# Attention a of a four-layer kernel: programs reordered in each step, and eight steps in a round of the loop

## The reference, cut to what matters

```python
topk = max(1, int(Tx * 0.3))                       # 76 of 256
qkv = x @ W_qkv.T + b_qkv                          # 16 heads of 8 features
scores = einsum('bhid,bhjd->bhij', q, k) * scale
topk_scores, indices = top_k(scores, topk)
masked = full_like(scores, -inf).at[..., indices].set(topk_scores)
out = einsum('bhij,bhjd->bhid', softmax(masked), v)
return out @ W_out.T + b_out
```

## Time and profile before

| what | us |
|---|---|
| median of 3 executions | 5544.91 (5527.25 to 5550.4) |
| the profiled execution's own time | 5548.73 |
| its span | 5547.0 |
| TensorE busy | 4738.9 (85%) |
| VectorE busy | 4094.9 (74%) |
| ScalarE busy | 3148.7 (57%) |
| GpSimd busy | 2516.4 (45%) |
| attention a in the span | about 90 to 2810 |

### The profile page before, as it was taken

The page is one execution under the profiler, slowest core; times in us unless marked ns, Lnnn a source line. Parts: engine busy times, 40 slices in busy tenths (PEclk is TensorE's granted clock), DMA queues, the critical chain, the costliest instruction groups (busy, mean ns, idle before and its releaser), DMA issues. The chain is left out here.

```text
span 5547.0 us, 121740 instructions
## 1 busy us (share of the span) xinstructions
PE 4738.9 (85%) x34686; PEld 3322.2 (60%) x34686; DVE 4094.9 (74%) x14487; ACT 3148.7 (57%) x10145; POOL 2516.4 (45%) x3026
## 2 busy tenths in 40 slices
PE   4578788788786887887889999989999998999998
PEld 2244444444443444444468888866666666888887
DVE  3788888888887888888958888855555554788886
ACT  3587777677775777777622222257667776222222
POOL 0465555565554555656644444421111111444444
PEclk6566665565665566667589999999999999999999
DMA  2000000000000000000023443410000000434344
GB/s 67 10 13 10 10 13 10 10 13 9 10 13 7 13 10 10 13 10 12 7 58 81 84 85 81 89 24 10 10 10 12 10 10 9 92 77 91 78 87 98
DMA packets 358589, 188.51 MB, mean 34 GB/s; under 512 B 190691, under 2 KB 346886, under 8 KB 358150
## 3 DMA queue, kind: packets, MB, share of 16 engines
q1 hardware_dynamic: 358150, 183.55, 16.4%
HBM read 147.04 MB, written 11.01 MB: 28 GB/s over the span
## 5 line engine op out<-in xcount | busy, mean ns | idle before, releaser
L845 ACT ACTIVATE junk<-SS,nt 128x256 bf16<-128x256 f32 x3072 | 1515.4, 502 | 188.4 <-POOL nt L481 113.3
L493 POOL TENSOR_SCALAR gone<-SS,mid 128x256 bf16<-128x256 f32 x1024 | 1193.0, 1180 | 664.3 <-DVEq L1039 533.2
L1206 POOL TENSOR_TENSOR f_hid<-f_g_m,f_cbs 128x256 f32<-128x256 f32 x1024 | 743.4, 726 | 853.2 <-DVE f_g_m L1451 660.6
L1306 ACT ACTIVATE f_th<-bank 128x256 f32<-128x256 f32 x1088 | 417.1, 383 | 1149.0 <-PE bank L1237 1149.0
L1236 PE MATMUL bank<-f_xTf,wgT 128*128 128x256 f32 x2176 | 692.3, 400 | 54.3 <-DVE f_g_m L1451 38.6
L668 PE MATMUL bank<-q4x,k4x 32*128 32x256 f32 x2048 | 526.2, 603 | 224.4 <-DVE SS L961 186.9
L1852 DVE TENSOR_REDUCE nmxb<-bank 128x2 f32<-128x512 f32 x512 | 330.1, 688 | 474.6 <-PE bank L1624 474.6
L1237 PE MATMUL bank<-f_xTf,wuT 128*128 128x256 f32 x2176 | 651.5, 381 | 0.0
L1268 PEld LDWEIGHTS bank<-wdT,f_hid 128*128 128x128 f32 x4096 | 601.5, 191 | 66.9 <-POOL f_hid L1206 12.5
L1268 PE MATMUL bank<-wdT,f_hid 128*128 128x128 f32 x4096 | 629.6, 276 | 10.5 <-POOL f_hid L1206 10.4
L845 ACT ACTIVATION_READ_ACCUMULATOR junk<-SS,nt 128x1 f32 x3072 | 599.5, 195 | 0.0
(11 more groups left out here) (233 smaller groups left out, 8134.9 us busy)
## 6 DMA issues: line engine op xcount, KB each, us to landing
f_cbs<-f_shares SPq DMA_DIRECT2D x512, 256.0 KB, 5.8
q4x<-q SPq DMA_DIRECT2D x64, 256.0 KB, 2.3
k4x<-k SPq DMA_DIRECT2D x64, 128.0 KB, 2.1
qrow<-q_rows SPq DMA_DIRECT2D x512, 8.0 KB
q_rows<-qTb SPq DMA_DIRECT2D x32, 128.0 KB, 1.7
out_dram<-xres SPq DMA_DIRECT2D x4, 1024.0 KB, 9.3
q4x<-nmx_rows SPq DMA_DIRECT2D x128, 4.0 KB
f_shares<-f_combT SPq DMA_DIRECT2D x64, 32.0 KB, 1.4
```

Of the source, the lines that this page charges most:

```text
L493: last = pool.tensor_scalar(gone[:, h % 4, i, :], SS[:, (u - lag) % 4, c, :], mid[:, (u - lag) % 4, c:c + 1], 0.0, ALU.subtract, ALU.min)
L845: nc.scalar.activation(junk[:, c % 2, :], SS[:, uu % 4, c, :], ACT.Sign, bias=bias(c), accum_out=acc[:, k, uu % 4, c:c + 1]).then_inc(s["s ...
L1206: pool.tensor_tensor(hid[:, e % NBUF, :], g_m[:, e % NBUF, :], cbs[:, par, e, :], ALU.mult).then_inc(s["hid"], 1)
```

## The change

1. `schedule` writes steps -1 to 7 out, runs steps 8 to 55 in 6 rounds of eight steps, and writes steps 56 to 67 out.
2. TensorE: in a quarter the four scores of the next group come first, then (quarter 2) `project(1)` or `spreads`, then `below_max` and `remove`, then `weigh` of the pair before (`SUMS`), then the guests. `turn_sums` moves from quarter 3 of a step to quarter 0 of the next, `turn_x` from quarter 1 to 0, `turn_o` from quarter 0 to 1, `q_rows` to quarter 0 behind `turn_sums`, `moments` and `queries` of the even step and `values` of the odd step behind `first_scores`.
3. ScalarE: the pairs of exponentials come at h = 2, 4, 6, 8 in place of 1, 3, 5, 7; the copy of the sums at h = 8 in place of 6, `oT` at 4 in place of 1, `take_qn` at 8 in place of 7, `take_v` at h = 8 of the odd step in place of h = 0 of the even one.
4. VectorE: `normalise` at h = 2 in place of 0, `take_k` at 7 in place of 6, `take_qr` at 3 in place of 2, `take_mom` at 5 in place of 4, the addition of y at 7 in place of 6.
5. GpSimd: `front` ahead of `outsiders(3, (6, 7))`.
6. The order of uses of M0 and M1 follows (`USES`): `gram` moves to M1, `oT` to M0.

```diff
-        USES = ({"v": 0, "xT": -1, "q0": -1, "q1": -1, "k": -1, "qn": -1, "gram": -1, "qtok": -1, "mom": -1},
-                {"f0": 1, "ktok": -1, "n0": 2, "oT": 2, "f1": 1, "y": 2, "n1": 1})
+        USES = ({"xT": -1, "q0": -1, "q1": -1, "k": -1, "qn": -1, "qtok": -1, "oT": 2, "mom": -1, "v": -1},
+                {"n0": 2, "f0": 1, "ktok": -1, "gram": -1, "n1": 2, "f1": 1, "y": 2})
...
-        BODY = (1, BATCH // 2 - 1)
+        SUMS = ((3, 0), (3, 2), (3, 4), (3, 6))
+        STEPS = 8
+        BODY = (1, GROUPS // STEPS - 1)
...
-            for u in range(4):
-                step(u, 0, u)
+            for t in range(STEPS):
+                step(t, t // 2, t % 4)
             with eng.Fori(*BODY) as i:
-                for u in range(4):
-                    step(i * 4 + u, i * 2 + u // 2, u)
...
+                for n in range(STEPS):
+                    step(i * STEPS + n, i * (STEPS // 2) + n // 2, n % 4)
+            for t in range(STEPS * BODY[1], GROUPS + 4):
+                step(t, t // 2, t % 4)
...
-                    outsiders(3, (6, 7))
                     if even and ahead:
                         front(bb + 1)
+                    outsiders(3, (6, 7))
...
-                        wait(pe, s["oc"], t - 2)
+                        wait(pe, s["oc"], t - 3)
                         use1(m1_before(bb, "n0" if even else "n1"))
...
-                        ahead = d < 3 and runs(t, -1)
-                        n = 2 * d + 2
-                        if ahead:
+                        if d < 3 and runs(t, -1):
+                            n = 2 * d + 2
                             free_bank(t + 1, n + 1)
+                            for i in range(HALVES):
+                                score(n, u + 1, i)
+                                score(n + 1, u + 1, i)
+                        if d == 2 and front:
+                            if even:
+                                project(1, m0_before(bb, "q1"))
+                            else:
+                                wait(pe, s["m1c"], m1_before(bb, "gram") + 1)
+                                spreads(m0_before(bb, "mom"))
                         if runs(g):
                             wait(pe, s["turned"], TURNED * (g + 1))
                             wait(pe, s["pt"], 8 * g + a)
-                        for k in range(2):
-                            if runs(g):
+                            for k in range(2):
                                 below_max(v, a, k)
                                 below_max(v, a + 1, k)
-                            if ahead:
-                                score(n, u + 1, k)
-                                score(n + 1, u + 1, k)
...
+                        late, a = SUMS[d]
+                        weigh(t - late, (u - late) % 4, a)
+                        if d == 0:
+                            if runs(t, 4):
+                                turn_sums()
+                            if front and even:
+                                turn_x(bb + 1, m0_before(bb, "xT"))
+                            if front and not even:
+                                q_rows(m0_before(bb, "qtok"))
+                        if d == 1:
+                            if not even and tail:
+                                turn_o()
+                            if runs(t, 2):
+                                judged()
+                            if front and even:
+                                project(0, m0_before(bb, "q0"))
+                        if d == 2:
+                            if front and even:
+                                k_rows(m1_before(bb, "ktok"))
+                                project(2, m0_before(bb, "k"))
+                            if not even and tail:
+                                project_o()
+                        if d == 3:
+                            if even and front:
+                                wait(pe, s["m0c"], m0_before(bb, "k") + 1)
+                            if runs(t, -2):
+                                first_scores(t + 2, u + 2)
+                            if even and front:
+                                moments(m1_before(bb, "gram"))
+                                queries(m0_before(bb, "qn"))
+                            if front and not even:
                                 values(m0_before(bb, "v"))
...
-                        if h % 2 == 1:
-                            late, a = PAIRS[h // 2]
+                        if h >= 2 and h % 2 == 0:
+                            late, a = PAIRS[h // 2 - 1]
                             exponentials(t - late, a)
                             exponentials(t - late, a + 1)
...
+                        if not even and front and h == 8:
+                            take_v(bb + 1, m0_before(bb, "v"))
+                        if h == 8 and runs(t, 3):
                             wait(act, s["pv"], 4 * (t - 2))
...
-                        if h == 0 and runs(t, 4):
+                        if h == 2 and runs(t, 4):
                             normalise()
...
-                        if front and even and h == 6:
+                        if front and even and h == 7:
                             take_k(m1_before(bb, "ktok"))
```

More of the change, by code:

```diff
@@ L389, in before @@
                 return b * len(order) + first - sum(max(lag, 0) for lag in order.values()) + list(order).index(what)
-            n = first
-            for c in range(b + 1):
+            n = 0
+            for c in range(-1, b + 1):
                 for o, lag in order.items():
@@ L626, in _ @@
                 k_rows(0)
-                wait(pe, s["m1c"], 1)
-                for n, f in enumerate((moments, q_rows, spreads)):
-                    f(5 + n)
+                q_rows(5)
+                moments(1)
+                wait(pe, s["m1c"], 2)
+                spreads(6)
+                values(7)
                 def rows(h):
@@ L685, in weigh @@
                             wait(pe, s["oc"], g)
-                            pe.wait_ge(s["vput"], bb)
+                            wait(pe, s["vput"], bb - 1 if even else bb)
                         for k in range(HALVES):
@@ L770, in step @@
-                        weigh(g, v, a)
-                        if even and front:
-                            if d == 1:
-                                project(0, m0_before(bb, "q0"))
-                            if d == 2:
-                                project(2, m0_before(bb, "k"))
-                            if d == 3:
-                                queries(m0_before(bb, "qn"))
-                        if not even and front and d == 0:
-                            wait(pe, s["m0c"], m0_before(bb, "qn") + 1)
-                            q_rows(m0_before(bb, "qtok"))
@@ L781, in step @@
-                    if even and front:
-                        wait(pe, s["m0c"], m0_before(bb, "k") + 1)
-                    if runs(t, -2):
-                        first_scores(t + 2, u + 2)
+                        late, a = SUMS[d]
[7 more added lines that the diff above has]
+                                q_rows(m0_before(bb, "qtok"))
@@ L822, in _ @@
                 take_qn(4)
+                take_v(0, 7)
                 own.end()
@@ L863, in step @@
                             count(t, k, u, bias, ready, done, range(CUTS[k][j], CUTS[k][j + 1]))
-                        if h == 0 and even and runs(bb, 0, BATCH):
-                            take_v(bb, m0_before(bb, "v"))
                         if even and front:
@@ L1020, in normalise @@
                     def normalise():
-                        n1 = m1_before(bb - 1, "n1") if even else m1_before(bb, "n0")
+                        n1 = m1_before(bb, "n0" if even else "n1")
                         wait(dve, s["m1"], n1 + 1)
```

81 lines of the change are left out of this document (24 added, 57 removed).

## The result

| | before | after |
|---|---|---|
| median, us | 5547.65 (5527.25 to 5553.43, 4 runs) | 5475.2 (5474.23 to 5481.61, 4 runs) |
| ratio | | 0.9878, 95% interval 0.9852 to 0.9905 |
| span of the profiled execution | 5547.0 | 5479.9 |

The account below looks back on a forecast made before the run. No engine fills a step: the engines wait for one another in turn, VectorE nearest to full. Savings of 43 + 43 + 27 + 88 = 201 us from 5548.7 gave 5348, or 5344 against the median; range 5253 to 5485.

Parts of the forecast that it names:

- only the first half is touched: Reading of the profile: the change affects only the first half of the span, attention a; no cost was forecast for later stages.
- rival 3: Whole kernel: only the longer round gains, rstd and k-row waits turning into waits for scores; 5502 us, chance 0.08.
- eight jumps fewer: Attention a's loop: six rounds jump back 5 times, not 13, at 5.4 us each; 43 us saved, bounds 26 to 43.
- wait for rstd: VectorE in attention a: with GpSimd's front ahead of outsiders, rstd comes 4.7 us earlier and all 43 us go.
- wait for k rows: VectorE in attention a: take_k one turn later removes the 27 us left after the jumps' share.
- wait for scores: VectorE in attention a: TensorE's new order leaves 66 of 154 us; 88 saved, bounds nothing to 154.
- Scores first and sums later: TensorE in attention a: second pair of halves ready after 2.1 us, not 4.6, and weigh no longer waits; 88 us saved.
- 29 us without a gap raise the clock: TensorE in even steps: gapless work lifts its clock, saving 3 us or more of a 5 us lateness.
- Rival 1: Attention a: VectorE is the only bound, so all waits for scores and hi_t go too; 5263 us, floor 5253, chance 0.17.
- Rival 2: Even steps of attention a: ScalarE becomes the bound, holding a pair of steps at some 77.0 us; 5439 us, chance 0.20.
- Rival 4: TensorE's quarter 0: turn_sums waits for osum and holds up the scores; slower, 5616 us, chance 0.06.
- Rival 5: VectorE and GpSimd in shorter steps: the shared port's lock costs some 30 us; 5374 us, chance 0.03.

## Why the prediction was wrong, and where it was right

**The step that failed** is in the first paragraph, "only the first half is touched", and with it, under the longer round, "the eight steps written out in place of rounds add nothing to the work, as the step after the exit shows". They add nothing where they stand. They move everything behind them: 148 us in the first experts (shown with waits on VectorE, in both kernels) and 59 in attention b (shown with waits on TensorE), 207 in all. The profile before could not show it, since its loops lay in good places; but the 3.3 us of "issue" behind each jump had a cause of this kind (in the trace after, 8 KB instruction packets lie around each of the five), and a change of code length should have raised the question of the other loops. No rival named it, and rival 3's 5502 would have been near for the wrong reason. That 5475 lies in the stated range is luck as well: the range was drawn for attention a alone, and 274 us gained there and 207 lost behind it happen to fall together inside it. By itself attention a (5275 with the later loops put back) is below the forecast's own 5300 to 5400.

**Attention a**, forecast -201, measured -274, term by term:

| term | forecast | measured |
|---|---|---|
| eight jumps fewer | 43 | 49 in the old order (rounds of eight alone), 29 in the new (rounds of four with the new order) |
| wait for rstd | 43 | the wait went from 42.9 to 0; undone, 73 |
| wait for k rows | 27, and 16 within the jumps | the wait fell by 39; not undone by itself |
| wait for scores | 88 | the wait fell by 120 |
| wait for hi_t | 0 | the wait fell by 15 |

The eight jumps held 16 us of the wait for k rows; in the new order that wait is gone by itself, so 24 to 29 us are left for the jumps, near the direct part of 26. The signs and the kinds of all terms were right. Of the 73 us by which the sum was too small, 32 are the scores, since the estimate of 66 us left there was too high (34 are), 15 are hi_t, and 18 are two waits that had no term, those behind onrm (9.6 to 0) and behind the branch (81.8 to 72.7). VectorE's idle time in attention a fell by 278 us in all (476.7 to 199.1), which is the stage's gain.

**turn_x** had no term. "ScalarE gains some 7 us of room. It needs it" was the right chain, but it was given no price; undone, it costs 77 us.

**Scores first and sums later** stood as one term. Apart they are very unlike: 16 to 20 us and 350 us. The reason given for the first, that scores are ready after 2.1 and not 4.6 us, was worth little; the runs point to the wait in `weigh` as what counted, with the reserve named at that run. Costs of undoing overlap and do not sum to the gain: 350 is more than all of it.

**The clock.** It rose from 0.62 to 0.64 only, not to the 0.65 looked for, and steps of 35.6 to 37.3 us came without it. The prediction's step "29 us without a gap raise the clock" is not borne out: in the step with the jump TensorE was busy for 36.82 of 39.94 us at a clock of 0.50, and ahead of the rise in the earlier trace rows it had been busy for 6.08 us of 2190 to 2200 and 4.05 us of 2200 to 2206, which is no stretch without a gap. The rule that the prediction cites from the Trainium skill ("TensorE: Matmul & The Clock Gate", Part 1), that sustained activity releases the throttle, does not agree with that step as the trace counts busy time, and it is not what removed the waits here.

**Rivals.** Rival 1 (VectorE the only bound, 5263) is what attention a became: with the code put back in place the kernel takes 5275. Rival 2 did not come: ScalarE's wait for the input of the exponentials fell from 277.7 to 219.0 us. Rival 3 did not: VectorE's wait for scores is 34 us. Rival 4 did not: TensorE's wait for osum ahead of `turn_sums`, 82 us before, is 0.7. Rival 5 did not either: L974's mean went from 511 to 515 ns, 4 ns in 1024, 4 us. The trace before says more on it: of 1024 L976, 474 begin while an L493 of GpSimd is under way, and they take 546 ns on average and 716 at most, against 479 for the 436 that meet none. The sign named for `turn_x` came: ScalarE's wait for it fell from 157.1 us in 30 waits to 17.5 in 12, the longest 1.8.

## What to carry to other kernels

A change of the length of a program moves every loop behind it on that engine, and a loop in a bad place can take back most of what the change gains (207 of 274 us here); so look at all stages, not only at the edited one, and above all for "issue" idle time at the first instruction of a loop's round. If it is there, a few instructions that do nothing, put ahead of the loop, can move it out, as they did here; that is worth trying in both directions before a change is judged. Within a stage, take a wait out of the queue of an engine that others depend on by giving the awaited work a whole turn more, and count what stands behind each wait, not the wait alone.

## What the runs showed of the hardware that was not expected

A loop of 272 instructions on VectorE costs nothing or 10.6 us at each jump, by 128-instruction blocks: bad at 52, 62 and 190, good at 26, 28, 44, 66 and 86. Its instructions come in packets of 8 KB, TensorE's in 16 KB. TensorE's loop of 1998 instructions fetched 10 or 11 packets in each round at all the places tried; its place made 0 to 59 us of 1020, growing over some 60 instructions and then gone, a good half of it a second stop behind the jump and the rest a lower clock. Waits that are already met cost next to nothing while they are few: with 46 on VectorE and 106 on TensorE attention a and the stages behind it take what they took in the better of the two kernels, each to within 5 us; 384 on TensorE cost 18 us. A VectorE instruction that reads two tensors of SBUF ran beside a GpSimd instruction that reads SBUF, in 546 ns on average in place of 479, and neither held the other up for its whole length.
